# The fc1 scales on another DMA queue, the work on them on another engine, and a reordered end of VectorE's list

## What is computed

```python
x = x + attn(layernorm(x))
x = x + ffn(layernorm(x))

# attn: four gates from one product, and a recurrence over the steps
pre = x @ W + b                          # 256 -> 1024
i, f, o, z = split(pre)
i = softcap(i + input_bias); f = -softplus(f); o = sigmoid(o); z = tanh(z)
m2 = max(f + m, i)
c = exp(f + m - m2) * c + exp(i - m2) * z
n = exp(f + m - m2) * n + exp(i - m2)
h = o * c / (n + 1e-6)
out = h / rms(h) * scale

# ffn: layer norm, gamma and beta, two products with weights from integers
w1 = (fc1_q - 128) * fc1_scales          # one scale per 128 rows and column
y = silu(h @ w1 + fc1_bias)              # 256 -> 1024
w2 = (fc2_q - 128) * fc2_scales
return residual + 0.5 * (y @ w2 + fc2_bias)
```

## Time and profile before

| | us |
|---|---|
| median of 3 runs | 313.07 |
| lowest and highest of them | 312.94 to 313.12 |
| the profiled execution, its own time | 313.88 |
| its span (first to last instruction of the profile) | 311.9 |
| TensorE busy | 295.4 (95% of the span) |
| VectorE busy | 265.1 (85%) |
| ScalarE busy | 233.3 (75%) |
| GpSimd busy | 126.5 (41%) |

### The profile page before, as it was taken

How to read it: one execution, slowest core, us unless ns; L and a number is a source line. 1 busy time by engine, 2 the same in 40 slices (tenths; PEclk the granted TensorE clock), 3 DMA queues, 4 the chain that set the end, 5 groups by cost and what they waited for, 6 DMA issues and landing times.

```text
span 311.9 us, 4767 instructions
## 1 busy us (share of the span) xinstructions
PE 295.4 (95%) x1728; PEld 255.2 (82%) x1728; DVE 265.1 (85%) x476; ACT 233.3 (75%) x376; POOL 126.5 (41%) x135
## 2 busy tenths in 40 slices
PE   8799999979899899999998999999999979989996
PEld 6578788856798689987896889988899869879886
DVE  3798989999899999999989998899979998863531
ACT  1599988789879985899694987699875777941930
POOL 0234057320182519611970159111999365154000
PEclk9999999799999999999999999999999999999999
DMA  7980003060000021003000110010000100200101
GB/s 267 344 295 7 0 1 69 0 134 0 2 1 2 12 76 51 0 34 103 1 2 34 39 64 0 0 39 31 1 2 0 67 2 0 69 0 2 68 0 67
DMA packets 11238, 14.73 MB, mean 47 GB/s; under 512 B 848, under 2 KB 10320, under 8 KB 10960
## 3 DMA queue, kind: packets, MB, share of 16 engines
q1 hardware_dynamic: 10368, 12.07, 11.4%
q0 software_dynamic: 288, 1.57, 2.5%
q10 hardware_dynamic: 560, 0.79, 0.7%
HBM read 8.67 MB, written 4.19 MB: 41 GB/s over the span
## 4 chain that ended last, share of the span: by engine, by line
PE 31%; DVE 22%; POOL 19%; issue 12%; ACT 11%; DMA 4%; ACTq 0%; POOLq 0%; DVEq 0%; SPq 0%
POOL rows L1156 4%; POOL g L1141 4%; ACT y L573 4%; PE mm_ps L236 4%; PE mm_ps L238 4%; PE mm_ps L237 4%; DVE y_lo L852 4%; PE z_ps L236 3%; PE z_ps L238 3%; PE z_ps L237 3%; DVE g L820 3%; POOL r L1134 2%; DVE rows L828 2%; DVE bn L833 2%; DMA s<-fc_scale_cols 2%
## 5 line engine op out<-in xcount | busy, mean ns | idle before, releaser
L236 PE MATMUL z_ps<-w_hi,y_hi 128*128 128x256 f32 x248 | 71.3, 288 | 2.4 <-DVE y_lo L852 2.4
L238 PE MATMUL z_ps<-w_hi,y_lo 128*128 128x256 f32 x248 | 70.0, 282 | 0.0
L237 PE MATMUL z_ps<-w_lo,y_hi 128*128 128x256 f32 x248 | 69.9, 282 | 0.0
L573 ACT ACTIVATE y<-mm_ps,b_all,unit 128x512 f32<-128x512 f32 x60 | 46.1, 769 | 11.4 <-PE mm_ps L329 9.7
L236 PEld LDWEIGHTS z_ps<-w_hi,y_hi 128*128 128x128 f32 x248 | 46.8, 189 | 4.0 <-DVE y_lo L852 3.7
L852 DVE TENSOR_TENSOR y_lo<-y,y_hi 128x512 fp32r<-128x512 f32 x64 | 42.8, 684 | 6.9 <-ACT y_hi L576 6.8
L237 PEld LDWEIGHTS z_ps<-w_lo,y_hi 128*128 128x128 f32 x248 | 46.9, 189 | 0.4
L238 PEld LDWEIGHTS z_ps<-w_hi,y_lo 128*128 128x128 f32 x248 | 46.8, 189 | 0.0
L322 PE MATMUL mm_ps<-gt_hi,w_hi 128*128 128x512 f32 x124 | 39.9, 403 | 1.6 <-ACT y L573 1.6
L236 PE MATMUL mm_ps<-xt_hi,wg_hi 128*128 128x512 f32 x96 | 38.4, 400 | 1.1 <-ACT f_gate L505 1.1
L576 ACT ACTIVATE y_hi<-y 128x512 fp32r<-128x512 f32 x60 | 37.9, 632 | 1.9
(11 more groups left out here) (176 smaller groups left out, 653.9 us busy)
## 6 DMA issues: line engine op xcount, KB each, us to landing
out<-rows SPq DMA_DIRECT2D x15, 256.0 KB, 2.1
rows<-x SPq DMA_DIRECT2D x7, 512.0 KB, 7.4
q<-fc_q SPq DMA_DIRECT2D x2, 1024.0 KB, 11.6
wg_raw<-fc_scales SPq DMA_DIRECT2D x1, 1024.0 KB, 6.4
w_lo<-q POOLq DMA_DIRECT2D x1, 1024.0 KB, 7.0
wg_raw<-w_gates SPq DMA_DIRECT2D x1, 512.0 KB, 6.4
wg_raw<-w_gates ACTq DMA_DIRECT2D x1, 512.0 KB, 6.6
w_lo<-q POOLq DMA_DIRECT2D x1, 512.0 KB, 4.7
```

Source lines behind the costliest of these rows:

```text
L236: pe.matmul(dst, wh[w_at], ah[a_at], start=start, stop=False)
L237: pe.matmul(dst, wh[w_at], al[a_at], start=False, stop=False)
L238: return pe.matmul(dst, wl[w_at], ah[a_at], start=False, stop=stop)
L573: act.activation(y[:, j % YBUFS], fc1_bank(c, j), ACT.Silu, bias=b1_all[:, j:j + 1], scale=unit[:, j:j + 1]).then_inc(silu_done, 1)
```

## The change

The DMA of `s1` moves from ScalarE's queue to the head of GpSimd's. All steps on the scales move to VectorE, between `ln1(0)` and `x_normalised(0)`, with a wait for `s1` in front; GpSimd keeps none of them. In the loop, for t = 5 and 6, `base_bias(t - 3)` moves from in front of `newton(t - 1)` to behind `h(t - 1)`. Behind the loop several entries of VectorE's and GpSimd's lists change places. In chunk 6 the high parts of the last two y tiles are made by VectorE (`y_high`), in chunk 7 those of every second tile (`y_split_last`). TensorE's and SyncE's lists stay as they are.

```diff
@@ ScalarE
-            act.dma_start(s1[:], fc1_scale_cols).then_inc(s1_in, 16)
...
             silu(6, range(0, 2))
             square_sums(7)
-            silu(6, range(2, KF))
+            silu(6, range(2, 6))
+            silu_alone(6, range(6, KF))
             g_high(7)
-            silu(7, range(KF))
+            for j in range(0, KF, 2):
+                silu(7, range(j, j + 1))
+                silu_alone(7, range(j + 1, j + 2))
@@ VectorE
+            def y_split_last(j):
+                c = CHUNKS - 1
+                if j % 2:
+                    dve.wait_ge(silu_done, at(c, 8, j + 1))
+                    dve.tensor_copy(y_hi[:, j], y[:, j % YBUFS]).then_inc(y_hi_own, 1)
+                    dve.wait_ge(y_hi_own, (j + 1) // 2)
+                else:
+                    dve.wait_ge(y_hi_done, at(c, 8, j // 2 + 1))
+                dve.tensor_tensor(y_lo[:, j], y[:, j % YBUFS], y_hi[:, j].bitcast(F32), ALU.subtract
+                                  ).then_inc(y_lo_done, 1)
...
             ln1(0)
+            dve.wait_ge(s1_in, 16)
+            dve.tensor_tensor(tiny[:], s1[:, 0], s1[:, 0], ALU.mult).then_inc(unit_step, 1)
+            dve.wait_ge(unit_step, 1)
+            dve.tensor_scalar(tiny[:], tiny[:], TINY * TINY, 2.0 * TINY, ALU.is_lt, ALU.mult).then_inc(unit_step, 1)
+            dve.wait_ge(unit_step, 2)
+            dve.tensor_tensor(unit[:], s1[:, 0], tiny[:], ALU.add).then_inc(unit_step, 1)
             dve.wait_ge(unit_step, 3)
             dve.reciprocal(per_unit[:], unit[:]).then_inc(ratio_step, 1)
             dve.wait_ge(ratio_step, 1)
             dve.tensor_tensor(ratio[:], s1[:, 1], per_unit[:], ALU.mult).then_inc(ratio_step, 1)
+            dve.tensor_tensor(share[:], tiny[:], per_unit[:], ALU.mult).then_inc(unit_step, 1)
+            dve.wait_ge(unit_step, 4)
+            dve.tensor_scalar(share[:], share[:], -1.0, 1.0, ALU.mult, ALU.add).then_inc(share_ready, 1)
             x_normalised(0)
...
                     o_times_c(t - 1)
-                    base_bias(t - 3)
                     newton(t - 1)
                     refined(t - 1)
                     g_low(t - 2)
                     h(t - 1)
+                    base_bias(t - 3)
                     final(t - 3, 0)
...
             input_times_z(7)
+            maximum(7, range(KD))
+            g_low(5)
             base_bias(4)
-            g_low(5)
-            maximum(7, range(KD))
             denominators(7, range(KD))
...
             y_low(5, range(1, 2))
-            final(4, 1)
             residual(6)
             y_low(5, range(2, 4))
             ln2_sums(6)
             y_low(5, range(4, 5))
             ln2(6)
+            final(4, 1)
             y_low(5, range(5, KF))
             numerators(7)
+            o_times_c(7)
+            newton(7)
+            refined(7)
+            g_low(6)
+            h(7)
             base_bias(5)
-            o_times_c(7)
-            newton(7)
-            g_low(6)
-            refined(7)
-            h(7)
             final(5, 0)
             final(5, 1)
-            y_low(6, range(0, 1))
-            base_bias(6)
-            y_low(6, range(1, 2))
+            y_low(6, range(0, 2))
             mean_square(7)
             y_low(6, range(2, 3))
             h_scaled(7)
+            residual(7)
             y_low(6, range(3, 4))
-            residual(7)
+            ln2_sums(7)
             y_low(6, range(4, 5))
-            ln2_sums(7)
             ln2(7)
-            y_low(6, range(5, KF))
+            y_low(6, range(5, 6))
+            for j in range(6, KF):
+                y_high(6, j)
+                y_low(6, range(j, j + 1))
+            base_bias(6)
             g_low(7)
             final(6, 0)
             final(6, 1)
             base_bias(7)
-            y_low(7, range(KF))
+            for j in range(KF):
+                y_split_last(j)
@@ GpSimd
+            pool.dma_start(s1[:], fc1_scale_cols).then_inc(s1_in, 16)
             pool.memset(ident[:], 0.0).then_inc(ident_ready, 1)
...
-            pool.wait_ge(s1_in, 16)
-            pool.tensor_tensor(tiny[:], s1[:, 0], s1[:, 0], ALU.mult).then_inc(unit_step, 1)
-            pool.wait_ge(unit_step, 1)
-            pool.tensor_scalar(tiny[:], tiny[:], TINY * TINY, 2.0 * TINY, ALU.is_lt, ALU.mult).then_inc(unit_step, 1)
-            pool.wait_ge(unit_step, 2)
-            pool.tensor_tensor(unit[:], s1[:, 0], tiny[:], ALU.add).then_inc(unit_step, 1)
             pool.wait_ge(half_ready, 1)
             ln1_root(0)
-            pool.wait_ge(ratio_step, 1)
-            pool.tensor_tensor(share[:], tiny[:], per_unit[:], ALU.mult).then_inc(unit_step, 1)
-            pool.wait_ge(unit_step, 4)
-            pool.tensor_scalar(share[:], share[:], -1.0, 1.0, ALU.mult, ALU.add).then_inc(share_ready, 1)
             ln1_root(1)
...
             base(4)
-            base(5)
             rms_root(6)
             ln2_root(6)
+            base(5)
             base(6)
```

More of the change, by code:

```diff
@@ L191, in layer @@
         fc1_done, silu_done = sem("fc1_done"), sem("silu_done")
-        y_hi_done, y_lo_done = sem("y_hi_done"), sem("y_lo_done")
+        y_hi_done, y_lo_done, y_hi_own = sem("y_hi_done"), sem("y_lo_done"), sem("y_hi_own")
         fc2_done, final_done = sem("fc2_done"), sem("final_done")
@@ L1067, in _ @@
             ln2(6)
+            final(4, 1)
             y_low(5, range(5, KF))
             numerators(7)
-            base_bias(5)
             o_times_c(7)
             newton(7)
+            refined(7)
             g_low(6)
-            refined(7)
             h(7)
+            base_bias(5)
             final(5, 0)
             final(5, 1)
-            y_low(6, range(0, 1))
-            base_bias(6)
-            y_low(6, range(1, 2))
+            y_low(6, range(0, 2))
             mean_square(7)
```

## The result

| | before | after |
|---|---|---|
| median of 7 runs | 313.07 us (312.35 to 313.14) | 311.32 us (309.81 to 311.77) |
| the profiled execution | 313.88 us, span 311.9 | 311.77 us, span 310.0 |
| mean granted clock of that execution | 0.995 | 0.988 |

The ratio is 0.9931, with a 95% interval of 0.9914 to 0.9948: faster, by 1.75 us between the medians (2.2 by the ratio) where 5.3 was forecast, and outside the range. The runs after also spread wider than those before, over 1.96 us against 0.79.

The account below looks back on a forecast made before the run. TensorE, busy for 95% of the span, was taken to bound the kernel. The terms -2.95 - 1.5 - 0.94 + 1.2 - 1.1 sum to -5.3, taking the median from 313.07 to 307.8 us, range 306.4 to 310.3.

Parts of the forecast that it names:

- The start, -2.95: Before the first gate matmul: with the scales there by 5.95, x is normalised from 7.5 on, 2.95 us earlier.
- rival 1: Start: the scales land late, at 7.2 to 8.2; the start brings 1.7 to 0.7, time 309.1 to 310.1; chance 0.17.
- so the rest follows at the same distance: Behind the start: chunk 1's x and fc1's weights land well in time, so everything later keeps the 2.95 us.
- The loop, -1.5: Loop's second pass: VectorE's wait for base in front of newton goes, so TensorE's transposes for h come 1.5 us earlier.
- Tail (a), -0.94: Chunk 6's transposes start at 255.1 instead of 256.04, despite TensorE's 2.3 us stand for final(4, 1): -0.94 us.
- rival 4: The clock: the stand in tail (a) or the shifted start brings another 3 us slow stretch, costing 1.5; 309.3; chance 0.06.
- I keep before's clock: Tail: its three terms are worked out on the before kernel's clock, with shifts noted against it.
- Tail (b), +1.2: Chunk 6: VectorE's longer stretch slows GpSimd's g_normalised(7), for which TensorE waits; +1.2 us, bounds 0 and +1.9.
- Tail (c), -1.1: Chunk 7: every second high part on VectorE lets fc2's first tile run its last k at 299.04, not 300.14; -1.1 us.
- Rival 2: Tail: the 2.3 us stand isn't made good, (a) is 0 and (b) 1.9; tail +0.8, time 309.4; chance 0.20.

Follow-up runs that it names:

- start_second: The kernel before with all steps on the scales on VectorE and the scales' load second on ScalarE's queue, behind the x rows; 310.78 us.
- loop_only: The kernel before with only the loop's edit, base_bias behind h; 312.23 us, ratio 0.9974.
- filler: The change with 8 dummy matmuls on TensorE in front of its wait for final(4, 1); 310.28 us, ratio 0.9910.
- final_back: The change with final(4, 1) put back in front of residual(6); 308.68 us, ratio 0.9867.
- act_norm: final_back with the normalised g of chunk 7 written by ScalarE instead of GpSimd; 307.06 us, ratio 0.9813.
- seven_norm: act_norm with chunk 7's fc1 tiles as before, ScalarE making silu and high part of every tile; 308.20 us, ratio 0.9849.
- start_loop: The kernel before with the change's start and loop edits and the old tail; 310.87 us, ratio 0.9928.
- fill7: final_back with six dummy products on TensorE between fc2_both(6, 0) and g_turned(7); 308.41 us, ratio 0.9861.
- lists_back: final_back with chunk 6 as before: both high parts on ScalarE, base_bias(6) between the two y_low(6) parts; 307.30 us, ratio 0.9814.

## Why the prediction was wrong, point by point

- **The start, -2.95: failed at the landing of the scales.** I took the row of the same queue, 4.7 us, over the row of the same load, 6.5. It was 5.9, issued at 1.26 and not at 0.7 (my bounds of 5.4 and 7.2 held it at the upper one). That is rival 1 at its earliest landing; the term was -2.04, 0.3 better than rival 1's since the seven steps on VectorE took 1.2 (7.22 to 8.42), not 1.5. The rest of the step was right: start_second, with the scales in time, shows x at 7.42 and -3.03. In the nine traces with the load on GpSimd's queue it took 5.3 to 5.9 us, and as second on ScalarE's 4.4. The Trainium skill, DMA: Bandwidth & Descriptors, table of specifications, gives GpSimd's path 0.4 us more to the first byte, which would have left the scales in time. These traces agree with it in direction and not in size, and no run separates set-up from place in the queue.
- **Not in the sum: 0.5 lost in front of `h_turned(2)`.** The step that failed is "so the rest follows at the same distance". One copy of VectorE's comes late in every trace with the new start (before, 0.11 behind the scan; there, 0.47 to 0.48). The cause stays open.
- **The loop, -1.5: mis-sized, -0.97.** The wait went, as forecast. It had also kept VectorE apart from `base`; 0.44 came back as slower steps. loop_only alone: -1.05 in its trace.
- **Tail (a), -0.94: the working held, and the clock took it.** On before's clock `ln2(6)` ended at 248.8 (forecast 248.9) and `final(4, 1)` at 249.4 (249.5). With 0.12 instead of 0.21 between matmuls for 3.41 us, the product would have ended about 1.5 sooner, at 255.0 (forecast 255.1). That is rival 4 (0.06), which named this stand. The step that failed is "I keep before's clock". filler, with the same wait but no stand, had no fall there; final_back, without the wait, moved the stage by 2.54, so even on a full clock the new place of `final(4, 1)` was the worse one.
- **Tail (b), +1.2: right, +1.27, in part by luck.** The four rows took 3.69 and not the 3.22 of chunk 4, and they began 0.24 sooner after `g_turned(6)` than before, not 0.16 later; the two misses cancel. One row in four was held, and the bound of +1.9 had all four held. The Trainium skill, SBUF — State Buffer, section "Who interferes with whom", says that where both engines want the ports that they share, the one that starts first shuts the other out for its whole instruction. The trace agrees for the row of 2.03, which ended 0.35 behind the bias sum; the rows ahead of it and behind it were not held.
- **Tail (c), -1.1: right, -1.20**, and 1.14 between the medians of act_norm and seven_norm.
- **The range.** Its upper end for the forecast itself was added up wrong: 307.8 + 0.7 for (b) + 0.6 for a loop of 0.9 is 309.1, not 308.9. The whole range, which went by the rivals, doesn't rest on it.

In sum the trace gives -1.97 at the last matmul: start 0.9 short, 0.5 lost on the way, loop 0.5 short, clock 1.4. Rival 2, that the tail gives its gain back, came true in its effect (start_loop has none of it and is as fast as the change), by rival 4's mechanism. I had priced the rivals one at a time. Rivals 1 and 4 came together: 307.8 + 0.9 + 1.4 is 310.1. The copy's 0.5, which stood nowhere, and the loop's 0.5 carried it over the range's end of 310.3.

What stays open, besides the copy: why the change's runs spread from 309.81 to 311.77, and why fill7 gained only 0.3 in the median. The executions without a trace list only a span and a mean clock, and a stretch of 3.41 us at half clock lowers the mean by 0.0055. In the eleven of before beside lists_back, a mean of 1.000 goes with spans of 310.3 to 310.5, one stretch with 311.1 to 311.2 (311.8 with the trace) and two with 311.3 to 311.4. So a stretch costs about 0.8 us there, where before's trace has it near 55 us, and 1.5 in the tail. What follows is an estimate from these numbers, since one execution of each kernel has a trace:

- The change. Six of its seven executions have a mean of 0.988 or 0.989, two stretches each, yet spans of 308.0, 308.3 and 308.4 or of 309.5, 309.5 and 310.0; the seventh, 0.983, has 309.9. The three short ones probably had no fall behind the stand. The landing of the scales adds to the spread: over the nine traces with GpSimd's queue, chunk 1's first transposes start between 18.50 and 19.08.
- final_back. Its trace, with the fall at 276, has a span of 307.4; the others have 306.6, 306.6, 306.9 and 308.4. So its median probably holds no such fall. That would also be why lists_back, act_norm and fill7, whose traces have none there, all came out 1.2 to 1.4 above the forecasts that had the end of this fall in them (305.9, 305.7 and 307.2).

That the place of the fall varies is shown: final_back and filler have one behind the hole of `g_turned(7)`, where after has none behind the same hole.

## What to carry to other kernels

A wait put in front of the engine that bounds the kernel costs its own length and can cost granted clock behind it; price the two together, even where slack downstream seems to cover the first. Before taking a wait away, look what it kept apart: here GpSimd's rows and VectorE's steps each grew once they ran side by side, and the stage gave back a third. For a small load that the first stage needs, take the duration of that load, not of its queue, and place it behind the loads that are needed sooner, ahead of the one needed later.
